# A graph network's edge sums on one core: chunks counted per 512-node group, in place of chunks counted per 2048 nodes

## The chip, the cores and the metric

One core of one Trainium2 chip runs the whole program. The metric is the device time of one execution in microseconds. Three runs of the kernel before took 5423.81, 5425.86 and 5426.53 us, so the median is 5425.86 us. One more execution was profiled; it took 5426.74 us, and its instructions span 5425.0 us.

## The reference, cut to what matters

The input is x with 50000 nodes of 128 features, and 100000 edges (src, dst) sorted by dst; 50000 of them are self loops, one per node, and the other 50000 have random ends. Four layers follow each other, each with a residual and a LayerNorm. They hold seven sums of neighbours' rows by destination node:

```python
msg = h[src] * norm[:, None]; out = segment_sum(msg, dst, n)       # two GCN layers
agg = segment_sum(h[src], dst, n) * inv_deg                        # three SAGE layers (the second 256 wide)
att = sigmoid(xs @ W_att[:d] + xd @ W_att[d:] + b_att)             # attention, then a GRU cell and a BatchNorm
aggregated = segment_sum((xs @ W_msg + b_msg) * att, dst, n)
neigh = segment_sum(x[src], dst, n); out = neigh @ W_neigh.T + b_neigh + x @ W_self.T + b_self
```

## The kernel before

The nodes are cut into T = 98 groups of 512 (`GRP`). Each of the seven stages with an edge sum (g1, g2 for GCN, s1, s2, s3 for SAGE, at for attention, cb for the last layer) is a loop over the 98 groups, written as a software pipeline: `over_groups` gives each engine its own list of steps with lags, and the engines meet through semaphores. `t` is the group, `r = t % 4` its place in a set of four.

A sort stage (`sort_and_scale`) runs first. It takes the self loops out of the edge list (they are added densely later), and ranks the other edges into slots of 128 edges, called chunks. K = 17 chunks serve a set of four groups (2048 nodes): 8 are filled from the set's first edge on, 8 from its last edge backwards, and the one in the middle takes what is left. Two tables come out: `idx` (which row to fetch for each of the 128 places of a chunk) and `dcol` (into which node column of the chunk's window it is to be added). As the number of edges that fall before a given node varies, the window of a chunk is wider than 128 nodes: `window(k)` adds `reach`, which grows with the root of the edges counted up to there. The windows are 168 to 344 columns wide and 4624 columns together.

In a stage, the path of a group's edge rows is this.

- `aim` (DVE, L830): copies the chunk indices of the group's batch to a small tile. `BATCH` deals the 17 chunks to the four groups as 5, 5, 4 and 3.
- `gather` (POOL, L840): one indirect DMA per chunk fetches 128 rows.
- `make_onehots` (DVE, L870): a comparison per chunk of the node numbers with `dcol` makes a one-hot matrix [128 edges x window]. In `at`, `open_` on ACT writes a sigmoid over the same window first, and `choose` on DVE masks it.
- In g1, s1 and s2 (`split=True`) the rows are split into a high half (`take_hi`, ACT) and a low half (`take_lo`, DVE), and PE multiplies each half in one pass. In g2, s3, at and cb PE multiplies fp32 rows, and the trace has two matmul records for each product.
- `sum_by_feature` (PE, L902, its matmuls on L909): for each piece of a chunk's window that falls in the group, one product rows x one-hot is added into the group's PSUM bank. `pieces(r)` lists them: a window that crosses a group's edge is cut in two pieces. Groups with r = 0 and r = 3 have 5 pieces (168, 224, 252, 196 and 80 columns, for r = 3 in reverse order), groups with r = 1 and r = 2 have 7 (80, 216, 312, 328, 232, 112 and 112, for r = 2 in reverse order).

The dense work of the layer follows on PE, ACT and DVE, and SP stores the result.

What sets the order around the change: POOL takes the gathers in order of the groups and waits for `aim`. `aim` waits until the place in the ring of rows is free: in the split stages for the split of the group four back; in the others, with two rings, for the sum of the group seven back (eight back for r = 3). On DVE, `aim` is the first step of each round (`on_vector`, L890); the one-hots of a group follow 2 to 4 rounds later. `free` makes the one-hots and the split wait for the sum of the group three back (four back for r = 3).

Of the kernel before, what the change touches and what calls it, by code (L numbers as in the profile page):

```python
# [9 lines left out]
F32 = mybir.dt.float32  # L10
# [19 lines left out]
SG = 4  # L30
SGN = SG * GRP
NSG = -(-T // SG)
K = 17
HALF = K // 2
SLOTS = NSG * K
BATCH = ((0, 5), (5, 10), (10, 14), (14, 17))
BATCHMAX = 5
EC = -(-EDGES // P)
# [3 lines left out]
LEAD = 16  # L42
CW = 832
COLS = CW // 32
OFFS = 7
# [13 lines left out]
assert LAST % BLK == 0 and T % SG == 2 and SLOTS * 4 <= 4 * 512 and LEAD + EC <= CW  # L59
# [7 lines left out]
def window(k):  # L67

    if k < HALF:
        a, b = P * k - reach(k), P * (k + 1) + reach(k + 1)  # L70
    elif k == HALF:
        a, b = P * k - reach(k), P * k + reach(k)
    else:
        m = K - 1 - k
        a, b = SGN - P * (m + 1) - reach(m + 1), SGN - P * m + reach(m)
    return max(a, 0), min(b, SGN)


LOW = [window(k)[0] for k in range(K)]
WIDE = [window(k)[1] - window(k)[0] for k in range(K)]  # L80
WMAX = max(WIDE)


def pieces(r, whole=True):


    got = []
    for k in range(K if whole else HALF):
        a, b = max(LOW[k], GRP * r), min(LOW[k] + WIDE[k], GRP * (r + 1))
        if a < b:  # L90
            got.append((k, a - GRP * r, b - GRP * r, a - LOW[k]))
    assert max(k for k, _, _, _ in got) < BATCH[r][1]
    return got
# [18 lines left out]
def first_slot(c):  # L112

    return (K * c >> 5) - 3
# [70 lines left out]
def build_program(nc, x, src, dst, w1, b1, w2, b2, ws0, wn0, sb0, ws1, wn1, sb1, ws2, wn2, sb2,  # L185
# [140 lines left out]
    def sort_and_scale():  # L326
# [3 lines left out]
        with ExitStack() as ctx:  # L330
# [11 lines left out]
            shift_i = tmp("shift_i", [P, 32], I32)  # L342
            e_f, bound, shift = tmp("edge_f", [P, CW]), tmp("bound", [P, CW]), tmp("shift", [P, 32])
            low, wide = tmp("low", [P, K]), tmp("wide", [P, K])
# [6 lines left out]
            above, front = tmp("above", [P, CW]), tmp("front", [P, CW])  # L351
            part, start = tmp("part", [P, COLS]), tmp("start", [P, COLS + 2])
            here, there, back = (tmp(n, [P, COLS]) for n in ("here", "there", "back"))
# [8 lines left out]
            filled = tmp("filled", [P, SLOTS])  # L362
# [20 lines left out]
            def by_block(tile):  # L383
                return tile[:, :].rearrange("p (j i) -> p j i", i=32)

            def spread(small):
                return small[:, 0:COLS].rearrange("p (j o) -> p j o", o=1).broadcast_to([P, COLS, 32])
# [5 lines left out]
            def _(pool):  # L393
                pool.iota(idxi[:, :], pattern=[[1, GRP]], base=0, channel_multiplier=0).then_inc(made, 1)
                pool.iota(e_i[:, :], pattern=[[P, CW]], base=-LEAD * P, channel_multiplier=1).then_inc(made, 1)
                pool.iota(bound_i[:, :].rearrange("p (j i) -> p j i", i=32), pattern=[[SGN, COLS], [0, 32]],
                          base=0, channel_multiplier=0).then_inc(made, 1)
                pool.iota(shift_i[:, :], pattern=[[K, 32]], base=368, channel_multiplier=0).then_inc(made, 1)
                pool.iota(cell_i[:, :], pattern=[[1, CW]], base=4, channel_multiplier=0).then_inc(made, 1)
# [4 lines left out]
                for k in range(K):  # L404
                    pool.memset(low[:, k:k + 1], float(LOW[k])).then_inc(made, 1)
                    pool.memset(wide[:, k:k + 1], float(WIDE[k])).then_inc(made, 1)
                pool.wait_ge(made, 9 + 2 * K)
# [4 lines left out]
            MADE = 12 + 2 * K  # L412
# [43 lines left out]
            def _(pe):  # L456
# [27 lines left out]
                for n in range(ROUNDS):  # L484
# [3 lines left out]
                    for c0 in range(n * PACK, min(n * PACK + PACK, EC)):  # L488
                        to, off = max(first_slot(c0), 0), first_slot(c0)
                        while to < min(off + OFFS, SLOTS):  # L490
                            upto = min(off + OFFS, SLOTS, (to // P + 1) * P)
# [55 lines left out]
            def _(dve):  # L547
# [18 lines left out]
                dve.memset(start[:, :], 0.0)  # L566
                dve.memset(cum[:, 0:1, :], 256.0)
# [7 lines left out]
                then(dve.tensor_scalar(shift_i[:, :], shift_i[:, :], 5, None, ALU.logical_shift_right))  # L575
# [3 lines left out]
                then(dve.tensor_scalar(shift[:, :], shift[:, :], -1.0, 22.0, ALU.mult, ALU.add))  # L579
# [20 lines left out]
                then(dve.tensor_scalar(i1[:, :], i1[:, :], SGN - 1, None, ALU.bitwise_and))  # L600
# [4 lines left out]
                then(dve.scalar_tensor_tensor(out=a[:, :], in0=a[:, :], scalar=float(SGN - 1), in1=loop[:, :],  # L605
# [6 lines left out]
                then(dve.scalar_tensor_tensor(out=c[:, :], in0=above[:, :], scalar=-float(SGN), in1=d[:, :],  # L612
                                              op0=ALU.mult, op1=ALU.add))
                then(dve.scalar_tensor_tensor(out=c[:, :], in0=c[:, :], scalar=float(SGN), in1=bound[:, :],
# [5 lines left out]
                for n, what in enumerate((s_t, c)):  # L620
# [12 lines left out]
                dve.tensor_tensor(there[:, :], start[:, 2:COLS + 2], start[:, 1:COLS + 1], ALU.subtract)  # L633
                then(dve.tensor_scalar(back[:, :], start[:, 1:COLS + 1], 1.0, None, ALU.subtract))
                dve.tensor_tensor(by_block(a), by_block(above), spread(here), ALU.mult)
                dve.tensor_tensor(by_block(b), by_block(above), spread(there), ALU.mult)
                then(dve.tensor_tensor(by_block(c), by_block(rank), spread(start), ALU.subtract))
                dve.tensor_tensor(b[:, :], b[:, :], rank[:, :], ALU.subtract)
                then(dve.tensor_tensor(c[:, :], c[:, :], a[:, :], ALU.subtract))
                dve.tensor_scalar(front[:, :], c[:, :], float(HALF * P), None, ALU.is_lt)  # L640
                then(dve.tensor_tensor(by_block(b), by_block(b), spread(back), ALU.add))
                then(dve.tensor_tensor(c[:, :], c[:, :], b[:, :], ALU.subtract))
                then(dve.tensor_tensor(c[:, :], c[:, :], front[:, :], ALU.mult))
# [11 lines left out]
                then(dve.tensor_scalar(b[:, :], a[:, :], 2.0, -float(K - 1), ALU.mult, ALU.add))  # L655
                dve.scalar_tensor_tensor(out=cell[:, :], in0=loop[:, :], scalar=FAR, in1=cell[:, :],
                                         op0=ALU.mult, op1=ALU.add)
                then(dve.tensor_tensor(b[:, :], b[:, :], front[:, :], ALU.mult))
                then(dve.tensor_tensor(b[:, :], b[:, :], a[:, :], ALU.subtract))
                then(dve.scalar_tensor_tensor(out=b[:, :], in0=above[:, :], scalar=float(K), in1=b[:, :],  # L660
                                              op0=ALU.mult, op1=ALU.add))
                then(dve.tensor_tensor(by_block(b), by_block(b), shift[:, :].rearrange("p (o i) -> p o i", o=1)
                                       .broadcast_to([P, COLS, 32]), ALU.add))
# [77 lines left out]
                for what, lo, hi in ((sums[0], 0, 3 * P), (sums[1], 3 * P, SLOTS)):  # L741
                    v = what[:, 0:(hi - lo) * 4].rearrange("p (s f) -> p s f", f=4)
                    dve.scalar_tensor_tensor(out=dsg[:, lo:hi], in0=v[:, :, 3], scalar=256.0,
                                             in1=v[:, :, 2], op0=ALU.mult, op1=ALU.add)
                    last = dve.scalar_tensor_tensor(out=dcol[:, lo:hi], in0=v[:, :, 1], scalar=256.0,
                                                    in1=v[:, :, 0], op0=ALU.mult, op1=ALU.add)
                then(last)
                dve.tensor_scalar(dsg[:, :], dsg[:, :], 256.0, None, ALU.subtract)
                then(dve.tensor_scalar(dcol[:, :], dcol[:, :], 256.0, 0.0, ALU.subtract, ALU.max))
                then(dve.tensor_copy(idx[:, :], dcol[:, :]))  # L750

                def by_slot(tile):
                    return tile[:, :].rearrange("p (g k) -> p g k", k=K)
# [1647 lines left out]
```

## Time and profile before

| | |
|---|---|
| median of three runs | 5425.86 us |
| profiled execution | 5426.74 us |
| its span | 5425.0 us |
| PE matmul busy | 4813.2 us (89%), 27901 instructions |
| PE weight loads | 3709.5 us (68%) |
| DVE | 3699.8 us (68%) |
| POOL | 3020.3 us (56%), 2962 instructions |
| ACT | 2719.8 us (50%) |

The stages follow each other with a barrier between them: sort from 0 to about 256 us, g1 to 858, g2 to 1414, s1 to 2017, s2 to 3344, s3 to 3925, at to 4665, a BatchNorm stage without edge sums to 4882, and cb to the end. The shares of the table are means over stages that differ: each stage has to be read by itself, with the windows view, and with the waits in it. "Busy" on PE overlaps from one matmul to the next, so the times between starts tell more of PE than the durations do.

### The profile page before, as it was taken

What the parts mean: (1) busy time and instruction counts of PE and PEld (TensorE: products, weight loads), DVE (VectorE), ACT (ScalarE), POOL (GpSimd) and SP (SyncE); (2) the same over time, 40 slices, a digit from 0 to 9 for tenths busy, and PEclk for the clock granted to TensorE, in tenths of its full rate; (3) what the DMA queues carried; (4) which work ended last, traced back from release to release, by engine and by line L of the source; (5) the groups of instructions that cost most, each with busy time, mean ns of one, the idle gap of its engine ahead of it and who ended that gap; (6) DMA issues with size and microseconds to landing.
All of it is one profiled execution on the core that took longest, in us unless ns stands there. A gap on an engine that the chain in (4) does not pass through costs nothing. (4 is left out here: it accounts for less than half of the span.)

```text
span 5425.0 us, 106083 instructions
## 1 busy us (share of the span) xinstructions
PE 4813.2 (89%) x27901; PEld 3709.5 (68%) x27901; DVE 3699.8 (68%) x11392; ACT 2719.8 (50%) x6654; POOL 3020.3 (56%) x2962
## 2 busy tenths in 40 slices
PE   4499996776699989999999998899799999888888
PEld 4488885665466657777777776777666666787877
DVE  8567775777566645555555554788678888786776
ACT  2644444777444442222222221787777777574555
POOL 0077775777677754444443442777475666007776
PEclk9999998888799999999999998999999999998999
DMA  4879995666599984444444443788877766694554
GB/s 147 280 240 274 274 274 172 199 198 197 196 316 319 319 296 158 157 160 164 161 160 157 162 163 99 216 251 248 242 224 224 224 216 219 221 340 133 156 149 142
DMA packets 575784, 1145.48 MB, mean 211 GB/s; under 512 B 113971, under 2 KB 120922, under 8 KB 572570
## 3 DMA queue, kind: packets, MB, share of 16 engines
q1 hardware_dynamic: 475802, 924.73, 50.1%
q0 software_dynamic: 99840, 219.14, 16.3%
q8 instruction: 55, 0.90, 0.1%
q14 instruction: 87, 0.71, 0.0%
HBM read 705.43 MB, written 438.05 MB: 211 GB/s over the span
## 5 line engine op out<-in xcount | busy, mean ns | idle before, releaser
L845 POOL DMA_INDIRECT s_rows<-t_h,s_index x416 | 530.5, 1275 | 761.3 <-DVE s_index L838 659.9
L845 POOL DMA_INDIRECT g_rows<-t_x,g_index x416 | 427.4, 1027 | 381.7 <-issue 362.6
L845 POOL DMA_INDIRECT cb_rows<-t_x,cb_index x416 | 395.1, 950 | 398.8 <-DVE cb_index L838 273.7
L845 POOL DMA_INDIRECT at_rows<-t_m,at_index x416 | 432.8, 1040 | 303.2 <-DVE at_index L838 190.6
L1767 ACT ACTIVATE s_hid<-bank,sb_c 128x512 f32<-128x512 f32 x196 | 124.1, 684 | 787.4 <-PE bank L1740 787.4
L845 POOL DMA_INDIRECT s_rows<-t_v,s_index x416 | 401.9, 966 | 207.3 <-issue 124.1
L845 POOL DMA_INDIRECT s_rows<-t_x,s_index x416 | 423.1, 1017 | 161.0 <-issue 120.5
L845 POOL DMA_INDIRECT g_rows<-t_h,g_index x416 | 403.4, 970 | 171.4 <-issue 124.4
L909 PE MATMUL bank<-s_onehot,s_hi 128*128 128x80 f32 (+9 forms) x1758 | 438.8, 289 | 49.5 <-DVE s_lo L880 46.2
L1804 DVE TENSOR_TENSOR s_rout<-bank,s_x 128x512 f32<-128x512 f32 x98 | 67.7, 691 | 534.9 <-PE bank L1752 534.9
L909 PE MATMUL bank<-s_onehot,s_lo 128*128 128x80 f32 (+9 forms) x1758 | 431.7, 285 | 0.0
L909 PE MATMUL bank<-g_onehot,g_rows 128*128 128x80 f32 (+9 forms) x1172 | 283.1, 403 | 148.0 <-DMA g_rows<-t_h,g_index 131.2
L1752 PEld LDWEIGHTS bank<-wuv_s,s_hid 128*128 128x128 f32 x3136 | 365.5, 192 | 47.4 <-issue 47.4
L873 DVE TENSOR_SCALAR s_onehot<-iota,dcol 128x276 fp32r<-128x276 f32 (+15 forms) x1248 | 386.5, 372 | 0.6
L909 PEld LDWEIGHTS bank<-s_onehot,s_hi 128*128 128x128 f32 x1758 | 341.3, 194 | 54.7 <-issue 46.3
L1740 PE MATMUL bank<-s_ht,ws_s 128*128 128x512 f32 x784 | 375.6, 601 | 0.0
L909 PEld LDWEIGHTS bank<-g_onehot,g_rows 128*128 128x128 f32 x1172 | 236.7, 232 | 193.4 <-issue 120.7
L1740 PE MATMUL bank<-s_agg,wn_s 128*128 128x512 f32 x784 | 368.4, 592 | 0.0
L1752 PE MATMUL bank<-wuv_s,s_hid 128*128 128x128 f32 x3136 | 366.0, 275 | 0.9 <-DVE s_rout L1804 0.9
L909 PEld LDWEIGHTS bank<-s_onehot,s_lo 128*128 128x128 f32 x1758 | 341.9, 194 | 0.7 <-issue 0.7
L880 DVE TENSOR_TENSOR s_lo<-s_rows,s_hi 128x640 fp32r<-128x640 f32 (+1 forms) x196 | 196.7, 1004 | 189.5 <-ACT s_hi L868 189.5
L909 PE MATMUL bank<-cb_onehot,cb_rows 128*128 128x80 f32 (+9 forms) x1172 | 246.3, 365 | 84.0 <-DMA cb_rows<-t_x,cb_index 83.5
(343 smaller groups left out, 12919.5 us busy)
## 6 DMA issues: line engine op xcount, KB each, us to landing
s_scale<-inv_d SPq DMA_DIRECT2D x196, 256.0 KB
htt<-s_ht SPq DMA_DIRECT2D x98, 512.0 KB
t_h<-s_hout SPq DMA_DIRECT2D x98, 512.0 KB
s_ht<-htt SPq DMA_DIRECT2D x98, 512.0 KB
t_m<-s_mout SPq DMA_DIRECT2D x98, 264.0 KB
at_own<-t_m SPq DMA_DIRECT2D x98, 264.0 KB
t_x<-so_x SPq DMA_DIRECT2D x98, 256.0 KB, 4.4
g_own<-t_x SPq DMA_DIRECT2D x98, 256.0 KB
```

The costliest lines, as they stand in the source:

```text
L845: pool.indirect_dma_start(out=self.rows[:, self.ring(q) + k, :], out_offset=None, in_=self.table[0:NPAD, :], in_offset=bass.IndirectOffset ...
L873: last = dve.tensor_scalar(self.onehot[:, k, 0:WIDE[k]], iota[:, 0:WIDE[k]], col(dcol, q.m * K + k), None, ALU.is_equal)
L880: return dve.tensor_tensor(self.lo[:, a:b, :], self.rows[:, a:b, :], self.hi[:, a:b, :].bitcast(F32), ALU.subtract)
L909: last = pe.matmul(to[:, a:b], part[:, at, h * P:(h + 1) * P], self.onehot[:, k, off:off + b - a], start=(i + s == 0), stop=(close and i + ...
L1740: last = pe.matmul(bank[4 + o][:, :], w[:, h, o * P:(o + 1) * P], r[:, h, :], start=(k + h == 0), stop=(k + h == 2))
L1752: last = pe.matmul(bank[6 + w][:, b * D:(b + 1) * D], hid[q.u][:, h, b * P:(b + 1) * P], wuv_s[:, h, w * D:(w + 1) * D], start=(h == 0), s ...
L1767: last = act.activation(hid[q.u][:, h, :], bank[4 + h][:, :], ACT.Relu, bias=sb1_c[:, h:h + 1])
L1804: dve.tensor_tensor(rout[q.u][:, :], bank[6][:, :], xin[q.u][:, :], ALU.add)\
```

## The change

Edges are ranked anew in each group of 512 nodes. A group has four chunks of its own, for its first 512 edges, with windows of 168, 224, 252 and 196 columns that lie all within the group. Edges from the 513th on go to a chunk that four groups share (chunk 0 of the set); in it each group has its own 80 columns, the last 80 nodes of the group. K stays 17 = 1 + 4 x 4, and the windows are 3680 columns together. `pieces(r)` now gives five pieces for every group, with the same columns as r = 0 had. `BATCH` deals 5, 4, 4 and 4. The last set, of two groups, has 9 chunks in place of 8.

The sort's arithmetic follows: 5 cells for each of 100 group places (500 in place of 425), a table 800 wide in place of 832, 6 offsets in place of 7 in the matmuls that move edges to their slots, and at the end the five cells of four groups are laid together into 17 slots. The shared chunk has two places in the one-hots and in the halves, and changes between them from set to set. `aim` of the two-ring stages moves to the end of DVE's round, and its waits change; so does the wait in `free`.

```diff
-K = 17
-BATCH = ((0, 5), (5, 10), (10, 14), (14, 17))
+KL = 5
+K = 1 + SG * (KL - 1)
+CELLS_ALL = NSG * SG * KL
+BATCH = ((0, 5), (5, 9), (9, 13), (13, 17))
+SPARE = 80
-LEAD = 16
-CW = 832
-OFFS = 7
+LEAD = 4
+CW = 800
+OFFS = 6
+def window(kl):
+    if kl == KL - 1:
+        return GRP - SPARE, GRP
+    return max(P * kl - reach(kl), 0), min(P * (kl + 1) + reach(kl + 1), GRP)
+def chunk(r, kl):
+    return 0 if kl == KL - 1 else 1 + r * (KL - 1) + kl
+def wide(k):
+    return SG * SPARE if k == 0 else WIDE[(k - 1) % (KL - 1)]
+def pieces(r):
+    return [(chunk(r, kl), LOW[kl], LOW[kl] + WIDE[kl], SPARE * r if kl == KL - 1 else 0) for kl in range(KL)]
...
+                dve.tensor_reduce(spare[:, :], by_four(node)[:, :, :, KL - 1], AX_X, ALU.add)
+                dve.tensor_copy(placed(idx)[:, :, 0], spare[:, :])
+                for r in range(SG):
+                    a1 = 1 + r * (KL - 1)
+                    dve.tensor_copy(placed(idx)[:, :, a1:a1 + KL - 1], by_four(node)[:, :, r, 0:KL - 1])
+                    last = dve.tensor_copy(placed(dcol)[:, :, a1:a1 + KL - 1], by_four(near)[:, :, r, 0:KL - 1])
...
+        def place(self, q, k):
+            if k == 0:
+                return 0 if q.e < SG else BATCH[0][1]
+            return k if k < BATCH[0][1] else k + 1
...
         def aim(self, dve, q):
...
-                    dve.wait_ge(self.summed, q.t - (7 if q.r == SG - 1 else 6))
+                    dve.wait_ge(self.summed, q.t - (4 if q.r == 0 else 7))
...
         def free(self, eng, q):
-                eng.wait_ge(self.summed, q.t - (3 if q.r == SG - 1 else 2))
+                eng.wait_ge(self.summed, q.t - 3)
...
-            over_groups(dve, [(0, lambda q: self.aim(dve, q))] +
-                        [(ahead + lag, stage) for lag, stage in stages])
+            aim = [(0, lambda q: self.aim(dve, q))]
+            rest = [(ahead + lag, stage) for lag, stage in stages]
+            over_groups(dve, aim + rest if self.halves else rest + aim)
...
-            todo = pieces(q.r, not (isinstance(q.t, int) and q.t >= T // SG * SG))
+            todo = pieces(q.r)
```

## Rows read from the trace of the kernel before

**Rows 1.** Windows view by stage: us, engines' busy (xcount), PEclk, DMA share, GB/s.

```profile
core 0: us, PE busy (x) PEld busy (x) DVE busy (x) ACT busy (x) POOL busy (x), PEclk, DMA share, GB/s
0.00:256.00 256.00, 117.31 (x1669) 112.94 (x1669) 189.56 (x297) 124.86 (x404) 6.09 (x50) 1.00 0.67 220
256.00:858.00 602.00, 578.42 (x3916) 483.27 (x3916) 442.85 (x1191) 279.61 (x686) 427.39 (x416) 0.99 0.86 259
858.00:1414.00 556.00, 379.66 (x1956) 324.95 (x1956) 373.46 (x1690) 374.85 (x1078) 403.36 (x416) 0.83 0.61 188
1414.00:2017.00 603.00, 571.13 (x2740) 373.36 (x2740) 351.27 (x808) 273.90 (x490) 423.12 (x416) 0.97 0.88 301
2017.00:3344.00 1327.00, 1306.57 (x7048) 930.71 (x7048) 742.73 (x1592) 281.12 (x392) 530.48 (x416) 0.99 0.48 157
3344.00:3925.00 581.00, 501.07 (x2936) 414.98 (x2936) 451.13 (x2082) 421.87 (x1176) 401.87 (x416) 0.94 0.77 226
3925.00:4665.00 740.00, 713.96 (x2936) 460.78 (x2936) 593.43 (x1203) 544.22 (x1299) 432.84 (x416) 0.98 0.67 213
...
4882.00:5425.00 543.00, 459.19 (x3132) 427.74 (x3132) 377.64 (x1690) 266.34 (x686) 395.11 (x416) 0.92 0.50 145
```

**Rows 2.** Groups by line on POOL: count, busy us, mean ns, idle before, releasers.

```profile
L845 POOL DMA_INDIRECT s_rows<-t_h,s_index x416 | 530.5, 1275 | 761.3 <-DVE s_index L838 659.9 <-issue 101.4
L845 POOL DMA_INDIRECT at_rows<-t_m,at_index x416 | 432.8, 1040 | 303.2 <-DVE at_index L838 190.6 <-issue 112.7
L845 POOL DMA_INDIRECT g_rows<-t_x,g_index x416 | 427.4, 1027 | 381.7 <-issue 362.6 <-DVE g_index L838 19.1
L845 POOL DMA_INDIRECT s_rows<-t_x,s_index x416 | 423.1, 1017 | 161.0 <-issue 120.5 <-DVE s_index L838 40.4
L845 POOL DMA_INDIRECT g_rows<-t_h,g_index x416 | 403.4, 970 | 171.4 <-issue 124.4 <-DVE g_index L838 47.0
L845 POOL DMA_INDIRECT s_rows<-t_v,s_index x416 | 401.9, 966 | 207.3 <-issue 124.1 <-DVE s_index L838 83.2
L845 POOL DMA_INDIRECT cb_rows<-t_x,cb_index x416 | 395.1, 950 | 398.8 <-DVE cb_index L838 273.7 <-issue 125.1
```

**Rows 3.** Waits view: who waited for whom, us in total, times, longest us.

```profile
POOL g_rows L845 <- issue: 487.1, 781, 249.2
POOL cb_rows L845 <- DVE cb_index L838: 273.7, 6, 272.2
ACT s_hout L1665 <- DMA t_h<-s_hout: 272.4, 89, 5.5
PE bank L909 <- DMA g_rows<-t_h,g_index: 131.2, 48, 17.6
PE bank L909 <- DMA cb_rows<-t_x,cb_index: 83.5, 31, 19.6
```

**Rows 4.** Timeline of PE in s2: first matmul of groups r = 0, 1, 2.

```profile
2609.49 0.33 PE L909 MATMUL bank<-s_onehot,s_hi 128*128 128x168 f32 x1
...
2622.18 0.28 PE L909 MATMUL bank<-s_onehot,s_hi 128*128 128x80 f32 x1
...
2636.04 0.30 PE L909 MATMUL bank<-s_onehot,s_hi 128*128 128x112 f32 x1
```

**Rows 5.** Timeline of PE in at: the sums of groups r = 2, 3, 0.

```profile
4306.47 2.62 PE L909 MATMUL bank<-at_onehot,at_rows 128*128 128x112 f32 x14
...
4314.15 1.81 PE L909 MATMUL bank<-at_onehot,at_rows 128*128 128x80 f32 x10
...
4320.98 1.76 PE L909 MATMUL bank<-at_onehot,at_rows 128*128 128x168 f32 x10
```

**Rows 6.** Timeline of s3: index of t = 24, sums of t = 19, gather of t = 24.

```profile
3461.15 0.16 DVE L838 COPY s_index<-idx 128x5 uint32 x1
3462.28 1.81 PE L909 MATMUL bank<-s_onehot,s_rows 128*128 128x80 f32 x10
...
3476.53 0.95 POOL L845 DMA_INDIRECT s_rows<-t_v,s_index  x1 [0.30 <-issue]
```

More of the change, by code:

```diff
@@ L350, in sort_and_scale @@
             a, b, c = (tmp(f"a{i}", [P, CW]) for i in range(3))
-            above, front = tmp("above", [P, CW]), tmp("front", [P, CW])
+            above, over = tmp("above", [P, CW]), tmp("over", [P, CW])
             part, start = tmp("part", [P, COLS]), tmp("start", [P, COLS + 2])
-            here, there, back = (tmp(n, [P, COLS]) for n in ("here", "there", "back"))
+            here, more, step = (tmp(n, [P, COLS]) for n in ("here", "more", "step"))
+            base = tmp("base", [P, COLS + 1])
             quad, cell = tmp("quad", [P, CW]), tmp("cell", [P, CW])
@@ L871, in make_onehots @@
             self.free(dve, q)
-            for k in range(*self.batch(q)):
-                last = dve.tensor_scalar(self.onehot[:, k, 0:WIDE[k]], iota[:, 0:WIDE[k]],
+            for k in range(*BATCH[q.r]):
+                last = dve.tensor_scalar(self.onehot[:, self.place(q, k), 0:wide(k)], iota[:, 0:wide(k)],
                                          col(dcol, q.m * K + k), None, ALU.is_equal)
@@ L878, in take_lo @@
             dve.wait_ge(self.split, q.t + 1)
-            a, b = self.batch(q)
+            a, b = self.span(q)
             return dve.tensor_tensor(self.lo[:, a:b, :], self.rows[:, a:b, :],
@@ L2062, in open_ @@
                     e.free(act, q)
-                    for k in range(*e.batch(q)):
-                        last = act.activation(e.onehot[:, k, 0:WIDE[k]],
-                                              asks[q.d % XS // SG][:, LOW[k]:LOW[k] + WIDE[k]], ACT.Sigmoid,
-                                              bias=e.rows[:, e.ring(q) + k, D:D + 1])
+                    for k in range(*BATCH[q.r]):
+                        ask = asks[q.d % XS // SG][:, :]
+                        hot = e.onehot[:, e.place(q, k), 0:width_of(q, k)]
+                        if k == 0:
+                            n = width_of(q, k) // SPARE
+                            ask = ask[:, 0:n * GRP].rearrange("p (r f) -> p r f", r=n)[:, :, GRP - SPARE:GRP]
+                            hot = hot.rearrange("p (r f) -> p r f", r=n)
+                        else:
+                            at = GRP * q.r + LOW[(k - 1) % (KL - 1)]
+                            ask = ask[:, at:at + wide(k)]
+                        last = act.activation(hot, ask, ACT.Sigmoid, bias=e.rows[:, e.row(q, k), D:D + 1])
                     last.then_inc(opens, 1)
```

198 lines of the change are left out of this document (104 added, 94 removed).

## Prediction

> **What bounds the kernel now.** I read the stages first, since the shares of the whole span are means over eight loops with different limits [rows 1]. PE is the fullest engine in all stages with an edge sum, but the fill differs: in s2 its records cover 1306.57 of 1327 us, in at 713.96 of 740, in g1 578.42 of 602, in s1 571.13 of 603. In g2, s3 and cb they cover 379.66 of 556, 501.07 of 581 and 459.19 of 543. The reader is to see two kinds of stage there.
>
> The groups of POOL come second [rows 2], for in the second kind the gathers have no air. In cb a gather takes 950 ns and the idle time of its "issue" kind is 125.1 / 416 = 0.30 us each, so 1.25 us per gather; 416 of them make 520 of the stage's 543 us, and the wait for an index is one long one before the stage began (272.2 of 273.7 us [rows 3]). In g2 it is (403.4 + 124.4) / 416 = 1.27 us, 528 of 556; in s3 (401.9 + 124.1) / 416 = 1.26 us, 526 of 581. What PE waits for there are the gathered rows [rows 3]. These three stages end when POOL has issued its last gather, plus a tail.
>
> In s2 and at it is the other way round: POOL waits 659.9 and 190.6 us for indices [rows 2], which come late because buffers come free late, and PE's starts show who sets the pace. In s2 the sums of r = 0 (five pieces, both halves, two feature halves) start at 2609.49 us, those of r = 1 (seven pieces) at 2622.18 and those of r = 2 at 2636.04 [rows 4]: 12.69 us after five pieces, 13.86 us after seven. In at it is 7.68 us after the seven pieces of r = 2 and 6.83 us after the five of r = 3 [rows 5]. A loop whose round grows by the length of its sums is bound by PE.
>
> g1 and s1 lie between. PE fills 96% and 95% of them, and POOL is close behind: in g1 its 427.4 us of gathers and 381.7 - 249.2 us of idle time (the 249.2 us [rows 3] are the sort) make 560 of 602 us, of which only 19.1 us are waits for an index.
>
> **The change part by part.**
>
> *Matmuls.* Per set of four groups the pieces go from 5 + 7 + 7 + 5 to 5 x 4, and the groups r = 1 and r = 2 get the very columns that r = 0 has now. So the rows price the change without a model: a group r = 1 or 2 will cost what r = 0 or 3 costs. There are 48 such groups in the 24 full sets (the last set has five pieces a group already).
>
> - s2: 13.86 - 12.69 = 1.17 us x 48 = 56 us, all on the path, since PE has the stage to itself.
> - at: 7.68 - 6.83 = 0.85 us x 48 = 41 us, on the path likewise. r = 3 and r = 0 follow each other now at the short round, so ACT (544.22 us) and DVE (593.43 us of 740) can follow; both lose columns too (4624 to 3680 of a set).
> - g1 and s1 sum one feature half where s2 sums two, with the same shapes: half of 1.17 us, 0.585 x 48 = 28 us each at most. POOL stands behind it. Without waits for an index a gather of g1 takes (427.4 + 381.7 - 249.2 - 19.1) / 416 = 1.30 us; 417 of them are 542 us, 18 less than the 560 of now. So g1 gives between 18 and 28, and I take 22. In s1 the same pace is (423.1 + 120.5) / 416 = 1.31 us, but there the DMA engines are the busiest of all gather stages (0.88, 301 GB/s) [rows 1], and ACT waits 272.4 us for stores [rows 3], in nearly every group (89 times). Below, that could leave 5; above, 28. I take 17.
> - g2, s3, cb: PE gets lighter by about 0.8 us in the same 48 groups (priced as in at, also fp32), but it waits for rows there; I take nothing.
>
> One rule decides whether POOL's pace in g1 holds. In cb the mean gather takes 950 ns, in g1, with the same 512-byte rows, 1027 ns [rows 2]. The Trainium skill's page "GPSIMD Engine Reference" (section 1, Specifications) says that GpSimd shares its SBUF interfaces with VectorE and meets contention from instructions with two SBUF inputs. By that rule the long gathers stay, since `take_lo` and the residual sums, which have two such inputs, stay; g1 would give 18. If the pace fell to cb's 1.25 us, PE would be the limit and g1 would give 28. No row here tells the two apart.
>
> *Gathers.* K stays 17; the last set fetches 9 chunks in place of 8. In the three stages that POOL bounds that is one gather more: 3 x 1.26 = 4 us. Elsewhere it hides under PE.
>
> *Index copies.* In g2, s3, at and cb `aim` moves to the end of DVE's round and for r = 0 it now waits for the sum of the group five back (seven before). Queued behind it are DVE's next round and, over the index, POOL's gathers. In s3 the index of t = 24 was copied at 3461.15 us, its gather started at 3476.53, and the sum that it will have to wait for ended at 3462.28 + 1.81 = 3464.09 [rows 6]: 12.4 us to spare for POOL. A DVE round later is 451.13 / 98 = 4.6 us later, 3465.8, which the wait then finds passed. In at POOL does start late, but at's PE has no use for rows that early; a round more (7 us) is what it costs POOL in lead. I take 0. Were the lead gone, each r = 0 batch would start late by what is missing: 1 us in one stage is 24 us.
>
> *`free`* waits for a sum at least as far back as before, so it can only loosen: 0.
>
> *One-hots, splits.* As many instructions, over 20% fewer columns, on engines that do not bind: 0. DVE sets the start of PE's sums now and then in s3, where it gets lighter.
>
> *Sort.* I count 18 DVE instructions more, net, mostly on 100 or fewer elements a partition, and the wide ones shrink by 32 of 832 columns. DVE's mean is 189.56 / 297 = 0.64 us [rows 1]; 18 of those would be +12 us, and 4% off all of its work is -7 us. The scaling of the last rows of x waits for DVE's tail, so part of it is on the path. The small ones are nearer to the bottom: I take +1 us.
>
> **The sum.** 56 + 41 + 22 + 17 = 136 us gained, 4 + 1 = 5 us lost: 131 us off the profiled execution's 5426.74 us (its span of 5425.0 and 1.7 around it), which is 5296 us. The median of the runs shown is 0.9 us below that execution, so the same number stands for it.
>
> **The rivals.**
>
> *g1 and s1 give nothing.* POOL and the transfers would hold them at 602 and 603 us, because POOL already takes 560 us of g1, nearly all of it work. For it: the long gathers. Against it: POOL still waits for indices, 19.1 and 40.4 us [rows 2], so it isn't quite the limit. Then 56 + 41 - 5 = 92 us: 5335 us.
>
> *The matmuls saved count in every stage.* If g2, s3 and cb were bound by PE after all, they would give 48 x 0.8 = 39 us each, 117 us more: 5179 us. For it: PE is their fullest engine [rows 1]. Against it: POOL's time alone nearly fills them, and the gathers are not fewer.
>
> *PE's clock falls where PE gets lighter, and the change costs time.* g2 has the emptiest PE (379.66 of 556 us) and a granted clock of 0.83, where s2, full, has 0.99 [rows 1]; s3 and cb have 0.94 and 0.92. The levels are 1.2 and 2.4 GHz. If 39 us less work put s3 and cb at the lower level throughout, PE's work there, now about 501 x 0.94 = 471 and 459 x 0.92 = 422 us at full clock, would be 2 x (471 - 39) = 864 and 2 x (422 - 39) = 766 us, and PE would bind them: +283 and +223 us, 375 net, or 5802 us. It decides against the change from about 0.26 of that on (131 of 506), at 5427 us. Against it: in cb PE with 85% busy records still has 0.92, and a PE at half clock would be busy all the time, which is the state in which s2 has 0.99. The Trainium skill's page "TensorE: Matmul & The Clock Gate" (section "HAM oscillation — how this bites in real kernels") describes this loss for loops that wait for DMAs between short bursts of matmuls; by it g2's 0.83 is expected, and less work per burst makes it worse.
>
> *The change doesn't do what it says.* If an edge fell outside its chunk's window, the kernel would take its general way, loops of 782 rounds with a gather and a scatter in each, and the time would be many milliseconds. Counted from the reference's inputs, the fullest group has 568 edges, so 56 over its 512, a set puts at most 79 on the shared chunk's 128 places, and none of those is a node below 459, where the window begins at 432.
>
> **How the numbers follow.** Forecast 0.78; g1 and s1 give nothing 0.12; all stages gain 0.03; the clock 0.04 (half of it past the point where it decides); the rest 0.03. The range takes the bounds of the unknown costs: at the low end 56 + 41 + 28 + 28 gained, the sort -7, 4 lost, 5271 us; at the high end the rival without g1 and s1 and a sort of +12, 5346 us. I give 5266 to 5344. What a measurement of this kernel can tell from no change is about 0.2%, 11 us: the first three cases and the half of the clock's before that point are faster by more than that, 0.95; of the other 0.05 I give 0.02 to the same time and 0.03 to a slower one.
>
> **What would show it.** After the change, PE's rounds in s2 should be 12.7 us for every r and 6.8 us in at; s2 should last about 1271 us, at 699, g1 580, s1 586; g2, s3 and cb should stay at 556, 581 and 543 within 3 us, with POOL's idle time free of new waits for an index in g2, s3 and cb. POOL's wait for indices should shrink in s2 and at. Wrong would be: rounds that still differ by r, a wait of ACT in at for gathered rows, POOL waiting for indices in cb, or a PE clock below 0.8 in s3 or cb.

## The result, and the profile after

The changed kernel takes 5292.36 us (median of 4 runs, 5287.13 to 5298.35) beside 5424.84 us for the kernel before on the same chip: a ratio of 0.9761, 95% interval 0.975 to 0.9773. Forecast were 5296 us and 5266 to 5344. The profiled execution took 5291.49 us, its span is 5289.7.

Stage lengths below are always taken from a stage's first gather to the next stage's first gather (cb to the end of the span), so that a row adds up to the span within 0.4 us. The column at + bn holds the BatchNorm stage too (some 216 us, see the view below). For the two kernels, in us:

| | sort | g1 | g2 | s1 | s2 | s3 | at + bn | cb |
|---|---|---|---|---|---|---|---|---|
| before | 255.9 | 604.8 | 555.6 | 603.3 | 1327.7 | 579.6 | 957.1 | 540.8 |
| after | 255.3 | 579.3 | 555.2 | 588.8 | 1270.3 | 583.7 | 915.5 | 541.3 |
| difference | -0.6 | -25.5 | -0.4 | -14.5 | -57.4 | +4.1 | -41.6 | +0.5 |
| forecast | +1 | -22 | +1 | -17 | -56 | +1 | -41 | +1 |

The windows view of the changed kernel, one row a stage as in [rows 1] (us, busy time of each engine, granted clock, DMA share, GB/s); at and bn have a row each here:

```profile
core 0: us, PE busy (x) PEld busy (x) DVE busy (x) ACT busy (x) POOL busy (x), PEclk, DMA share, GB/s
0.00:255.50 255.50, 116.89 (x1660) 112.40 (x1660) 187.55 (x309) 124.00 (x404) 6.08 (x30) 1.00 0.68 220
255.50:832.00 576.50, 550.30 (x3724) 452.53 (x3724) 430.87 (x1199) 287.09 (x686) 417.52 (x417) 0.99 0.88 270
832.00:1388.00 556.00, 351.84 (x1764) 316.14 (x1764) 366.98 (x1691) 373.09 (x1078) 403.98 (x417) 0.80 0.61 188
1388.00:1977.00 589.00, 548.69 (x2548) 346.17 (x2548) 341.29 (x809) 274.48 (x490) 420.52 (x417) 0.97 0.89 308
1977.00:3247.00 1270.00, 1249.64 (x6664) 873.51 (x6664) 730.51 (x1593) 281.52 (x392) 520.79 (x417) 0.99 0.50 165
3247.00:3831.00 584.00, 468.83 (x2744) 391.18 (x2744) 445.52 (x2083) 421.52 (x1176) 405.80 (x417) 0.94 0.75 225
3831.00:4530.00 699.00, 672.64 (x2744) 430.95 (x2744) 567.69 (x1199) 520.08 (x1300) 442.01 (x417) 0.98 0.71 225
4530.00:4746.00 216.00, 185.88 (x1568) 180.31 (x1568) 179.83 (x845) 153.09 (x443) 0.00 (x0) 0.95 0.91 328
4746.00:5289.70 543.70, 417.68 (x2940) 399.65 (x2940) 367.28 (x1691) 265.39 (x686) 396.13 (x417) 0.93 0.48 145
```

PE lost matmuls in every stage with an edge sum (192 in g1, s1, g2, s3, at and cb, 384 in s2), but only four stages became shorter. In g2, s3 and cb PE's busy time fell by 28, 32 and 42 us against [rows 1] and the stage stayed: there POOL's gathers fill the time as before. The granted clock moved little (0.80, 0.94 and 0.93, beside 0.83, 0.94 and 0.92).

The groups of POOL by line and shape answer to [rows 2]:

```profile
L881 POOL DMA_INDIRECT s_rows<-t_h,s_index x417 | 520.8, 1249 | 714.0 <-DVE s_index L874 614.9 <-issue 99.1
L881 POOL DMA_INDIRECT at_rows<-t_m,at_index x417 | 442.0, 1060 | 270.1 <-DVE at_index L874 160.9 <-issue 109.2
...
L881 POOL DMA_INDIRECT g_rows<-t_x,g_index x417 | 417.5, 1001 | 375.5 <-issue 362.4 <-DVE g_index L874 13.1
...
L881 POOL DMA_INDIRECT cb_rows<-t_x,cb_index x417 | 396.1, 950 | 381.3 <-DVE cb_index L874 256.3 <-issue 125.0
```

The waits for an index fell where PE sets the pace (s2 659.9 to 614.9, at 190.6 to 160.9). In the waits view (in all, times, longest), cb's is still the one long wait before its stage began, ACT's wait for s1's stores stayed, and one of at is new: before, ACT waited 20 us in all there.

```profile
POOL cb_rows L881 <- DVE cb_index L874: 256.3, 7, 254.4
...
ACT s_hout L1703 <- DMA t_h<-s_hout: 265.3, 92, 4.3
...
ACT at_n L2147 <- DVE at_mix L2179: 152.3, 98, 3.4
```

PE's timeline, first matmul of the sums of three groups in a row in s2 and then in at, answers to [rows 4, 5]. A round is the time from one group's first matmul to the next group's. The rounds are 12.70 and 12.68 us, and 6.83 and 6.82 us, whatever the group's number; 12.69 and 6.83 us is also the median for each of the four:

```profile
2605.24 0.32 PE L947 MATMUL bank<-s_onehot,s_hi 128*128 128x168 f32 x1
...
2617.94 0.32 PE L947 MATMUL bank<-s_onehot,s_hi 128*128 128x168 f32 x1
...
2630.62 0.33 PE L947 MATMUL bank<-s_onehot,s_hi 128*128 128x168 f32 x1
...
4299.47 1.76 PE L947 MATMUL bank<-at_onehot,at_rows 128*128 128x168 f32 x10
...
4306.30 1.76 PE L947 MATMUL bank<-at_onehot,at_rows 128*128 128x168 f32 x10
...
4313.12 1.76 PE L947 MATMUL bank<-at_onehot,at_rows 128*128 128x168 f32 x10
```

### The profile page after: what moved, and what is told of

Its sections match the earlier page's. It is cut to its first block and busy times, and to the rows that moved or that the text cites. A ratio compares the mean times of both kernels' runs of the same rounds, so it can differ in the third digit from the quotient of the medians.

```text
span 5289.7 us, 103008 instructions
## 1 busy us (share of the span) xinstructions
PE 4562.4 (86%) x26356; PEld 3502.8 (66%) x26356; DVE 3617.5 (68%) x11417; ACT 2700.3 (51%) x6655; POOL 3012.8 (57%) x2949
## 5 line engine op out<-in xcount | busy, mean ns | idle before, releaser
L881 POOL DMA_INDIRECT s_rows<-t_h,s_index x417 | 520.8, 1249 | 714.0 <-DVE s_index L874 614.9
L881 POOL DMA_INDIRECT g_rows<-t_x,g_index x417 | 417.5, 1001 | 375.5 <-issue 362.4
L881 POOL DMA_INDIRECT at_rows<-t_m,at_index x417 | 442.0, 1060 | 270.1 <-DVE at_index L874 160.9
L947 PE MATMUL bank<-g_onehot,g_rows 128*128 128x168 f32 (+4 forms) x980 | 241.1, 408 | 198.3 <-DMA g_rows<-t_h,g_index 198.1
L947 PE MATMUL bank<-s_onehot,s_hi 128*128 128x168 f32 (+4 forms) x1470 | 351.1, 282 | 57.0 <-DVE s_lo L915 52.1
L947 PEld LDWEIGHTS bank<-g_onehot,g_rows 128*128 128x128 f32 x980 | 215.9, 243 | 231.3 <-issue 165.8
L908 DVE TENSOR_SCALAR s_onehot<-iota,dcol 128x252 fp32r<-128x252 f32 (+9 forms) x1251 | 358.1, 349 | 8.5 <-PE bank L947 5.8
L947 PE MATMUL bank<-s_onehot,s_lo 128*128 128x168 f32 (+4 forms) x1470 | 338.8, 281 | 0.0
L947 PEld LDWEIGHTS bank<-s_onehot,s_hi 128*128 128x128 f32 x1470 | 285.6, 194 | 66.9 <-issue 53.0
L947 PE MATMUL bank<-cb_onehot,cb_rows 128*128 128x168 f32 (+4 forms) x980 | 195.8, 351 | 126.0 <-DMA cb_rows<-t_x,cb_index 120.4
L947 PE MATMUL bank<-s_onehot,s_rows 128*128 128x168 f32 (+4 forms) x980 | 200.3, 357 | 107.5 <-DMA s_rows<-t_v,s_index 104.2
## 6 DMA issues: line engine op xcount, KB each, us to landing
s_scale<-inv_d SPq DMA_DIRECT2D x196, 256.0 KB
t_x<-so_x SPq DMA_DIRECT2D x98, 256.0 KB, 4.4
g_own<-t_x SPq DMA_DIRECT2D x98, 256.0 KB
```

Of the source, the lines that this page charges most:

```text
L881: pool.indirect_dma_start(out=self.rows[:, self.row(q, k), :], out_offset=None, in_=self.table[0:NPAD, :], in_offset=bass.IndirectOffsetOn ...
L908: last = dve.tensor_scalar(self.onehot[:, self.place(q, k), 0:wide(k)], iota[:, 0:wide(k)], col(dcol, q.m * K + k), None, ALU.is_equal)
L947: last = pe.matmul(to[:, a:b], part[:, at, h * P:(h + 1) * P], self.onehot[:, self.place(q, k), off:off + b - a], start=(i + s == 0), stop ...
```

## The experiments

All start from the changed kernel; times are medians beside the kernel before on the same chip. Stage lengths of each profiled execution, us:

| | sort | g1 | g2 | s1 | s2 | s3 | at + bn | cb |
|---|---|---|---|---|---|---|---|---|
| after_again | 258.1 | 580.0 | 557.8 | 588.9 | 1270.3 | 579.3 | 912.0 | 541.8 |
| seven | 257.0 | 593.8 | 553.7 | 597.1 | 1316.0 | 584.1 | 915.8 | 541.2 |
| narrow | 256.0 | 578.8 | 558.2 | 596.9 | 1270.3 | 581.1 | 920.1 | 541.2 |
| extra_gather | 258.4 | 607.2 | 587.5 | 611.8 | 1270.2 | 612.0 | 920.2 | 572.7 |
| four | 253.9 | 580.0 | 557.3 | 589.1 | 1225.4 | 583.3 | 917.5 | 541.0 |
| aim_first | 255.9 | 578.9 | 555.8 | 588.8 | 1268.5 | 585.5 | 919.0 | 539.0 |
| hn4 | 258.2 | 577.2 | 552.1 | 591.0 | 1271.2 | 578.0 | 912.8 | 539.7 |
| hn4_four | 258.7 | 576.6 | 556.9 | 589.3 | 1225.0 | 581.7 | 889.5 | 539.8 |
| cand_four | 258.1 | 577.3 | 551.4 | 589.6 | 1224.7 | 584.0 | 891.4 | 540.3 |
| hout4 | 254.6 | 578.2 | 556.0 | 591.1 | 1270.3 | 579.2 | 914.7 | 540.2 |
| both4 | 260.1 | 579.5 | 555.4 | 580.4 | 1271.6 | 585.6 | 911.4 | 540.6 |
| best | 257.6 | 578.3 | 555.1 | 581.5 | 1271.2 | 585.9 | 912.2 | 542.4 |

**after_again** is the yardstick: the changed kernel as it is.

> The kernel after the change, once more, beside best on the same chip: 5287 to 5298 us as before. It says how far a single stage moves between runs of one kernel: the theories of the other runs rest on differences of 5 us or more.

5290.97 us (5279.35 to 5296.93), ratio 0.9751 [0.9735, 0.9767]. Stages that do the same work differ by up to 4.4 us from the first trace of this kernel (s3), s2 by nothing. Two traces make the scatter look small: over the six traces whose code for these stages is the same (after, after_again, hn4, hout4, both4, best) g2 spans 5.7 and s3 7.9 us, g1, s2 and cb no more than 2.8.

### What the saved matmul time was paid for

**seven** splits two windows, so that products are added and no columns.

```diff
...
+        if r in (1, 2) and kl in (1, 2):
+            mid = (a + b) // 2
+            got += [(chunk(r, kl), a, mid, off), (chunk(r, kl), mid, b, off + mid - a)]
...
```

> The middle two windows of the groups r = 1 and 2 are each cut in halves: seven products a group again in 48 groups, on the same 920 columns. The question is what the saving in s2 and at was paid for. Theory A (columns): the 1.2 and 0.85 us of a group came from the columns, 1392 before and 920 now; then s2 stays at 1270 us within 5 and at at 699 within 10, and the whole is within 20 us of 5292. Theory B (products): a product has a price of its own, whatever its width; then s2 gets back 40 us or more of its 58, at some 20 to 40 of its 41, g1 and s1 up to 20 each, and the whole is 5360 to 5420 us. PE's round after a group of r = 1 or 2 in s2 tells them apart: 12.7 us by A, 13.6 or more by B.

5357.27 us, 0.9875 [0.9854, 0.9896]. s2 gave back 45.7 us: theory B there. The timeline of PE in s2 shows it group by group (first matmuls of the sums; the first interval follows a group with five products, the second one with seven):

```profile
2639.30 0.32 PE L955 MATMUL bank<-s_onehot,s_hi 128*128 128x168 f32 x1
...
2651.99 0.32 PE L955 MATMUL bank<-s_onehot,s_hi 128*128 128x168 f32 x1
...
2665.56 0.33 PE L955 MATMUL bank<-s_onehot,s_hi 128*128 128x168 f32 x1
```

12.69 us after five products, 13.57 after seven; these are the medians over the stage too. A product more in the window list is 4 matmuls (two parts, two feature halves), so 0.88 us for 8 matmuls, 0.11 us each. g1 (+14.5) and s1 (+8.3) paid too; at (+0.3) did not, against B: its round after seven products is 6.92 us beside 6.83, so two products cost it only 0.09 us.

**narrow** is the counterpart: fewer columns, the same products.

```diff
-... LOW[kl] + WIDE[kl] ...
+... LOW[kl] + (WIDE[kl] if kl == KL - 1 else WIDE[kl] // 2) ...
```

> The other half of the question of seven: the same products (five a group), but the four wide windows are summed at half their width, 500 columns a group in place of 920; half of the edges' sums are left out, the one-hots and gathers stay. Theory B (a product has a price of its own): from seven, 48 groups with 8 products more cost s2 45.7 us, 0.119 us a product, which leaves 0.22 of the 1.17 us of a group for 1888 columns; the 1680 columns less here would then give at most 0.2 us in each of 98 groups, s2 1250 to 1270. Theory A (columns): 1.07 us a group, s2 about 1165. g1, s1, g2, s3, cb (POOL) and at (see hn4) stay within 5 us by either.

5299.56 us, 0.9755 [0.974, 0.977]. s2 is 1270.3 us, to the tenth what it was, and its round 12.67 us. Nearly half of the columns are gone from these sums, and nothing is gained: theory A is out for s2. The expected stages stayed within 5 us too, but for s1's 8 us, which I can't explain: 5.5 of them lie between POOL's first and last gather there, and s1's granted clock is 0.97 in both.

The starts of PE's weight loads fit that. First s2 after the change, then s2 before, where the products of 328 and 312 columns are:

```profile
2617.91 0.19 PEld L947 LDWEIGHTS bank<-s_onehot,s_hi 128*128 128x128 f32 x1
2618.02 0.19 PEld L947 LDWEIGHTS bank<-s_onehot,s_lo 128*128 128x128 f32 x1
2618.13 0.19 PEld L947 LDWEIGHTS bank<-s_onehot,s_hi 128*128 128x128 f32 x1
```

```profile
2636.79 0.19 PEld L909 LDWEIGHTS bank<-s_onehot,s_lo 128*128 128x128 f32 x1
2636.95 0.19 PEld L909 LDWEIGHTS bank<-s_onehot,s_hi 128*128 128x128 f32 x1
2637.10 0.19 PEld L909 LDWEIGHTS bank<-s_onehot,s_lo 128*128 128x128 f32 x1
2637.24 0.19 PEld L909 LDWEIGHTS bank<-s_onehot,s_hi 128*128 128x128 f32 x1
```

Every product loads its gathered rows as weights, and a load starts 0.11 us after the one before (now and then 0.12), under products of 80 to 252 columns alike; only behind the wide ones of before it is 0.15. So the 1.17 us of a group were 8 matmuls at 0.11, 0.88 us, and two windows too wide to hide behind a load, 8 matmuls at 0.035, 0.28 us: 1.16 us. The 0.11 us is not a price of every matmul: in the sort, matmuls with bf16 weights, each with a load of its own, start 0.06 us apart.

```profile
186.84 0.21 PE L499 MATMUL bank<-so_value,so_parts 128*128 128x24 bf16 x1
186.90 0.21 PE L509 MATMUL bank<-so_count,so_parts 128*128 128x16 bf16 x1
```

That it is the load of f32 weights that sets it is a reading of these starts; no run separates the load from another fixed price of a matmul on f32 rows.

at's sums are plain fp32, two matmul records for each product, and there the columns carry more of it: the matmuls of PE's gates (512 columns, two records) start 0.86 us apart, 1.67 ns a column, and the five windows with their 920 columns would take 920 x 1.67 ns = 1.54 of the 1.60 us that the sums last. The Trainium skill's page "FP8 and Floating Point Precision" (TensorE Precision Notes) has true fp32 as four passes through the array; 1.67 ns is four columns' time at 2.4 GHz, so the trace agrees. But the same 0.11 us a record stands under it: in narrow, with 500 columns (0.83 us at that price), the sums of at last 1.15 us from their first matmul to the next one of PE,

```profile
4297.44 1.31 PE L948 MATMUL bank<-at_onehot,at_rows 128*128 128x84 f32 x10
4298.59 1.10 PE L2076 MATMUL bank<-id_own,at_mine 128*128 128x128 f32 x8
```

and in narrow and seven the records of 84 to 126 columns start 0.11 to 0.14 us apart, those of 224 and 252 columns in seven 0.19 and 0.21.

### Which engine holds which stage now

**extra_gather** adds 25 gathers to every stage.

```diff
...
-            for k in range(a, b):
+            again = [(a, q.e // SG + (K + 1 if self.halves else 2 * K))] if q.r == 0 else []
+            for k, at in [(k, self.row(q, k)) for k in range(a, b)] + again:
...
```

> The first chunk of every set is fetched a second time, into a place that nothing reads: 25 gathers more in each stage. The theory behind the prediction: where POOL bounds the stage, each costs its whole pace of 1.25 to 1.27 us, so g2, s3 and cb become 31 us longer each (586, 615, 572); s2 and at, bound by PE, change by less than 5. g1 and s1 are the open places: if the change has brought them to POOL's pace, they grow by some 32 us as well; if PE still sets their round, by less than 10. Rival: the wait for a batch's rows and not POOL's issue sets the end in g2, s3 and cb, and a gather more in one batch of four is made up in the next three: less than 10 us there. The whole: 5385 us with g1 and s1 at PE's pace, 5450 with both at POOL's, 5300 by the rival.

5442.03 us, 1.0035 [1.0022, 1.0048]. g2 +32.3, s3 +28.3, cb +31.4, that is 1.29, 1.13 and 1.26 us a gather; s2 0, at +4.7. POOL bounds the first three and not the last two. g1 grew by 27.9 and s1 by 23.0, so the change has brought them to POOL's pace, nearly: from POOL's first gather to its last g1 takes 27.2 and s1 30.7 us more, and in s1 the tail behind the last gather is 7.9 us shorter. The added gathers move rows as well as take POOL's time, and no run parts the two; POOL's waits for an index did not grow. seven shows the other side: with two products more in half of the groups g1 pays 14.5 us of some 21 (half of 0.88 us in 48 groups, as g1 sums one feature half), so PE stands right behind POOL there.

**four** takes one product from every group.

```diff
-... for kl in range(KL)]
+... for kl in range(KL - 1)]
```

> The sums leave out the shared chunk's product (the edges of a group beyond 512); its rows are still gathered and its one-hot still made. Four products a group, on 756 of 920 columns. If PE bounds s2 and at, both get shorter again: by the columns, 1.2 us for 472 columns in s2 is 0.4 us for these 164, 40 us over 98 groups; by the products, 1.2 us for two is 0.6 for one, 59 us; in at 29 or 42. g2, s3 and cb stay within 5 us if POOL bounds them. g1 and s1: under 5 us each if POOL or the stores have become their limit, half of what s2 gains (20 to 30) if PE still is. The rival of the clock: PE gets lighter once more in g2, s3 and cb; if less work there can bring the lower clock, these stages show a granted clock clearly below 0.80, 0.94 and 0.93, and become longer.

(The expectation has the columns wrong: the shared chunk's window is 80 of the 920 columns, so theory A had 20 us for s2, and narrow has since refuted it.) 5239.5 us, 0.9657 [0.9636, 0.9679]. s2 -44.9 us, or 0.458 us a group, 0.11 us for each of its 4 matmuls: the same price a third time. g1 and s1 did not move: not PE. g2, s3 and cb kept their time and clock (0.80, 0.93, 0.93). But at did not move either (+2.0), and that was against the prediction, by which PE sets its round. narrow says the same: PE's sums are 0.45 us shorter there in each group, and at lasts 675.9 us from PE's first matmul to its last, beside 675.3.

**hn4** takes DVE's waits for stores out of at.

```diff
-            hn = ph.pair("hn", [P, GRP])
+            hn = ph.pair("hn", [P, GRP], n=3)
...
-            stored = ph.sems("stored")
+            stored = ph.sems("stored", 4)
...
-                return kept_slab(kept, q) if q.d % KEEP == 0 else hn[q.u][:, :]
+                return kept_slab(kept, q) if q.d % KEEP == 0 else hn[q.r - 1][:, :]
...
-                    if not is_first(q.t):
-                        dve.wait_ge(stored[q.u], q.n * 16)
+                    if not is_first(q.t, 4):
+                        dve.wait_ge(stored[q.r], q.m * 16)
```

> at gets four places for the new h and its stores in place of two. In the run four, at did not gain although PE had a product less in every group, so PE does not set at's round after the change, against the prediction's reason. Theory: DVE's round does, with its 5.8 us of work a group and its waits for the stores of h (24.5 + 20.9 + 15.8 = 61 us in the stage); ACT's 137 us of waits for the blend follow from it. Without the store waits at gets shorter by 15 to 40 us, until PE is the limit again (its records cover 673 of 699 us), and ACT waits less for the blend. Rival: a round trip between ACT and DVE sets it, the stores only fill its gaps: under 5 us. All other stages within 3 us.

5284.81 us, 0.9733 [0.9718, 0.9749]. at is 912.8 us: 2.7 less than in the first trace of the changed kernel, 0.8 more than in the second. The forecast gain of 15 to 40 us did not come. But the waits changed hands. The waits view over 600 us of at, first the changed kernel, then hn4:

```profile
ACT at_n L2147 <- DVE at_mix L2179: 137.3, 87, 3.4
...
DVE kept L2188 <- DMA hnt<-at_hn: 24.5, 21, 1.9
DVE at_hn L2188 <- DMA hnt<-at_hn: 20.9, 22, 1.6
DVE at_hn L2188 <- DMA hnt<-kept: 15.8, 22, 1.6
```

```profile
ACT at_agg L2134 <- PE bank L2075: 122.2, 83, 1.7
...
DVE at_mix L2175 <- ACT at_z L2142: 56.8, 64, 1.5
```

The stores are gone from it, and ACT now waits for PE's sums, as it did before the change (142.3 us in all). That looks like two limits at the same height, where taking one away meets the other; the next two runs test it.

**hn4_four** joins hn4 and four; **cand_four** is four with another way out, ACT's order:

```diff
-over_groups(act, [(4, hold), (6, candidate), (1, open_), (2, weigh), (5, gate)], XS)
+over_groups(act, [(4, hold), (1, open_), (6, candidate), (2, weigh), (5, gate)], XS)
```

> The four places of hn4 together with the four products a group of four (the edges beyond 512 of a group are left out of the sums). Open after hn4: at gained only 3 us, but ACT's largest wait there went from DVE's blend back to PE's sums. Theory X (a crossing): in the kernel after the change PE's round and DVE's round with its store waits are level in at; each experiment took away one of them and met the other. Then both together gain what neither did: in the run four PE's rounds without a stall were 6.68 us against 6.83, so 0.15 x 98 = 15 us, at 895 to 903 in place of 917 (four) and 913 (hn4). Theory R (a round trip of ACT and DVE, candidate to gate to blend to candidate): at stays at 910 to 917.

> Four products a group as in four, and ACT's tanh of the candidate comes after its sigmoids for the edges in place of ahead of them, so that the blend has 1.5 us more before ACT needs it; the stores keep two places. Theory R: the round trip is broken, at 890 to 905 us in place of 917. Theory X: DVE still waits for its stores every round, at 910 to 920.

5216.04 us, 0.9613 [0.9598, 0.9627], and 5216.56 us, 0.961 [0.9595, 0.9625]. at is 889.5 and 891.4 us, 28.0 and 26.1 less than in four. hn4_four went 5 us below theory X's range, cand_four fell into theory R's, and neither stayed where the other theory had it: the store waits are not the whole of it (cand_four keeps 37 us of them in the same window and gains all the same), nor is the round trip alone. With four products both edits shorten one chain, ACT's candidate to DVE's move with its store waits to the blend to the next candidate, and either is enough to bring it below PE's round. (The later candidate alone, with five products, was not run.) PE's sums in at, first in four, then in hn4_four:

```profile
4152.96 1.66 PE L947 MATMUL bank<-at_onehot,at_rows 128*128 128x168 f32 x8
...
4159.64 1.58 PE L947 MATMUL bank<-at_onehot,at_rows 128*128 128x168 f32 x8
...
4167.38 1.66 PE L947 MATMUL bank<-at_onehot,at_rows 128*128 128x168 f32 x8 [0.97 <-issue]
...
4174.06 1.58 PE L947 MATMUL bank<-at_onehot,at_rows 128*128 128x168 f32 x8
```

```profile
4153.89 1.58 PE L947 MATMUL bank<-at_onehot,at_rows 128*128 128x168 f32 x8
...
4160.49 1.58 PE L947 MATMUL bank<-at_onehot,at_rows 128*128 128x168 f32 x8
...
4167.10 1.58 PE L947 MATMUL bank<-at_onehot,at_rows 128*128 128x168 f32 x8
...
4173.70 1.58 PE L947 MATMUL bank<-at_onehot,at_rows 128*128 128x168 f32 x8
```

In four one round of each set, the one behind the sums of r = 0, is some 0.8 us longer (7.74 here, 7.40 the median), in hn4_four every round is 6.61. A set of four groups takes 27.3 us in the changed kernel, 27.6 in four, 27.7 in narrow and 26.4 in hn4_four (medians): PE's round counts only where the chain lets it. The total of a wait does not show which of the two holds the stage. In hn4_four ACT still waits for the blend in nearly every group:

```profile
ACT at_n L2147 <- DVE at_mix L2179: 122.7, 97, 3.2
```

**aim_first** undoes the place of the index copies.

```diff
-            over_groups(dve, aim + rest if self.halves else rest + aim)
+            over_groups(dve, aim + rest)
```

> The index copies stand ahead of DVE's round again in g2, s3, at and cb, as before the change, with the waits that the change gave them. The prediction took nothing for their place: g2, s3, at and cb then stay within 5 us of 555, 584, 699 and 541. Rival: the copy now waits for a sum so near that at the head of the round it holds up DVE's whole round, in at the blend that ACT and PE wait for; then at grows by 25 us or more (1 us in each set) and ACT's wait for the blend, 152 us now, grows with it; g2, s3 and cb, which have no such chain, less.

5291.71 us, 0.9757 [0.9737, 0.9777]. g2, s3 and cb within 2.3 us, at +3.5 (7.0 above after_again): the place is worth nothing that shows, and the rival's 25 us are out.

**hout4** asks whether stores hold s1.

```diff
-            hout = ph.pair("hout", [P, BLK * HID])
+            hout = ph.pair("hout", [P, BLK * HID], n=4)
...
-                        act.wait_ge(stored[q.u], q.n * 16)
+                        act.wait_ge(stored[q.r], q.m * 16)
...
```

> s1 gets four places for the rows that it stores, two before. Of the 28 us that the matmuls could give, s1 gave 14. Theory S (stores): ACT's copy-out waits 265 us for the store two groups back, holds up the split behind it, and with it DVE and PE; then s1 gains 8 to 14 us, and ACT's wait for the stores nearly goes. Theory P (POOL): extra_gather made s1 23 us longer, so POOL's pace holds it; then s1 stays within 5 us of 589, though ACT's waits go. Other stages within 3 us.

5286.12 us, 0.9734 [0.9719, 0.9749]. s1 is 591.1 us, and ACT's wait for the stores only became one for PE (waits view of hout4 in s1):

```profile
ACT s_hout L1703 <- PE bank L1680: 188.2, 86, 5.2
```

That is theory P. But both4 and best have the same code in s1 and took 580.4 and 581.5 us, 8 and 7 less, near theory S's lower end. The traces part s1 into POOL's first to last gather and a tail: 547 and 42 us in after and after_again, 555 and 36 in hout4, 548 and 32 in both4, 548 and 33 in best. So the tail was shorter in all three, and in hout4 longer gathers took it back; but four, with its stores as before, has 554 and 35. With one execution of each I leave it open.

### A kernel that beats both

**both4** joins hn4 and hout4; **best** adds the order of cand_four, with all five products.

> hn4 and hout4 in one kernel, the candidate to beat both: the two touch different stages, so their gains add up. By the theories above at gains 15 to 40 us and s1 0 to 5 (P) or 8 to 14 (S): 5240 to 5277 us in all; by the rival in at and P, 5288 to 5292.

> hn4, hout4 and the later candidate in one kernel with all five products, the candidate to beat both kernels. PE is the limit of at in hn4 already and POOL of s1, so theory X gives at 908 to 914 us and the whole 5276 to 5290; theory R gives at 890 to 905 and 5262 to 5275.

both4: 5285.29 us, 0.9725 [0.9711, 0.9738], between the two ranges expected of it: at gained nothing that shows (911.4 us), s1 8 us, and s3 was 2 to 6 us longer. best: 5276.16 us (5270.74 to 5286.31), 0.9723 [0.971, 0.9736], beside after_again's 0.9751 [0.9735, 0.9767] on the same chip. From the five times of each, best is 13 us faster than the changed kernel, with a 95% interval of 4 to 22 us. Where these are can't be read from the traces: best's profiled execution was its slowest (5286.31 us), and s1's 7 us less are nearly eaten by s3's 7 more. at is at PE's round of 6.83 us in it, as theory X has it.

## Why the prediction was right, and where its reasons were not

- **s2, 56 us: 57.4.** PE sets the round and prices the group; the rounds are level at 12.69 us. The reading that a change to the very shapes of r = 0 needs no model of a product held, and it had to: the step never said what is paid for. Columns would have given the same by accident: 472 of 1392 are 34%, and 34% of the 3.41 us that a group's seven products lasted are 1.16. seven and narrow show that it is the count; the starts of the weight loads add the two windows above 300 columns.
- **at, 41 us: 41.6** (45.1 by after_again). The same reading, and right in size. That PE alone sets the round was wrong: 6.83 us is level with the chain through ACT and DVE. "ACT and DVE can follow" held with nothing to spare, which busy times of 544 and 593 of 740 us didn't show. One product less, and the step would have failed (four). That the size came out is in part luck: the working had no more than two short rounds in a row (r = 3 and r = 0) as a sign that the chain could keep up in all four.
- **g1, 22 of 18 to 28: 25.5.** POOL is the limit now, as said. Its pace fell, but not to cb's: (417.5 + 375.5 - 248.6 - 13.1) / 417 = 1.27 us, between the 1.30 and the 1.25 weighed; 417 of these are 531 us, and 13 of waits make the 544 from its first gather to its last; the tail behind it shrank from 44.9 to 34.9 us. So POOL's part gave 15.5 us and the tail 10.0; the sum had no term for the tail, so that the two together come near its 22 is in part luck. By the rule in the Trainium skill's "GPSIMD Engine Reference" (section 1, Specifications) 18 us were due: the two-input instructions stayed, and of its 108 gathers over 1 us 92 stayed. The traces don't contradict its direction: after the change 84% of the gathers over 1 us in s3 lie beside the sum that makes `s_z`, which has two SBUF inputs, and 23% of the others; in g2 it is 76% and 25% for `g_z`. They don't show the cause either: the statistics that read `s_z` right behind it have one input and lie beside 84% and 18%, and in g1 itself `take_lo` lies beside 43% and 30%. No run took such instructions away.
- **s1, 17 of 5 to 28: 14.5.** The stores were named as what could hold it. extra_gather shows POOL's gathers instead (23.0 of the 31 us that 25 of them cost elsewhere); for the stores the runs disagree. The term was a choice inside wide bounds, so its nearness to 14.5 says little.
- **g2, s3, cb, 0 and 1.26 us for a gather each: -0.4, +4.1, +0.5**, or by the mean of both traces +0.9, +1.9 and +0.8. The second rival, that PE counts everywhere, is out.
- **Index copies and `free`, 0:** aim_first agrees. **Sort, +1:** -0.6 and +2.2 in the two traces, below what they can tell.
- **The clock:** the rival did not come. Lighter sums did go with a lower granted clock in g2 (0.83 before, 0.80 after, 0.67 in narrow), less in s3 (0.94, 0.94, 0.90) and cb (0.92, 0.93, 0.88), and the stages stayed (windows view of narrow, g2, s3 and cb):

```profile
835.00:1393.00 558.00, 345.84 (x1764) 314.55 (x1764) 368.74 (x1693) 375.56 (x1078) 406.34 (x417) 0.67 0.62 187
3260.00:3841.00 581.00, 430.83 (x2744) 353.28 (x2744) 446.01 (x2083) 420.70 (x1176) 403.86 (x417) 0.90 0.78 226
4762.00:5302.00 540.00, 395.72 (x2940) 383.53 (x2940) 364.71 (x1685) 267.07 (x686) 394.33 (x417) 0.88 0.51 146
```

POOL's gathers (406, 404 and 394 us with about 0.3 us behind each) hide a PE at that clock.

## What to carry to other kernels

Where groups of two kinds already alternate in one loop, the difference of their rounds prices turning one into the other, without a model of the instructions; but it holds only down to the next limit, and neither busy shares nor the total of a wait say how near that is. Before a sum is made cheaper, see in the starts of its matmuls and weight loads whether a product or its columns are paid for: in s2 narrower windows gained nothing and fewer ones did. An experiment that finds no gain can mean that something else is level, and not that the thing removed was cheap: take both away.

## What the runs showed that I had not expected

A matmul of s2's sums costs 0.11 to 0.12 us from 80 to 252 columns, and the same sum in plain fp32 in at pays 1.67 ns a column, but no less than about 0.11 us for each of its two records. In at PE's round and the ACT and DVE chain lay within a few us of each other over the whole stage, so that shortening either alone (four, hn4) moved it by 2.7 us at most from the first trace of the changed kernel and both (hn4_four, cand_four) by 24 to 26. And a granted clock of 0.67 cost g2 nothing that shows: 558.2 us beside 552.1 to 557.8 in the six traces of the unchanged stage.
